# GNN and expert layers on one core: 70 instead of 77 edge groups in the dense part, a ring of 14 slots for the edge sums, three matrix scatter-adds per expert tile

## The chip, the cores and the metric

The kernel runs on one core of a Trainium2 chip. The metric is the device time of one execution in microseconds (us), and the median of several executions is compared. The program is written engine by engine: TensorE (PE) multiplies, VectorE (DVE) and ScalarE (ACT) work on rows, GpSimd (POOL) issues the indirect DMAs (gathers and scatter-adds), SyncE (SP) issues most of the plain DMAs.

## What is computed

```python
x (6250, 256); 100000 edges (src, dst, edge_weight), sorted by dst; dst is 6250*u*u, so low nodes have many edges
# layer 0, graph part: sum of weighted neighbours, two products with batch norm and relu, residual
agg = segment_sum(edge_vals[:, None] * x[edge_col], edge_row)
# layer 0, experts: router, top 2 of 8 experts, each LayerNorm -> 256x1024 -> gelu -> 1024x256, residual
# layer 1, graph part, twice (c1, c2), with the same edges:
h   = relu(x @ w1 + b1)
agg = segment_sum(ew[:, None] * h[src], dst)
h   = relu(batch_norm(agg @ w2 + b2))
# layer 1, experts: small shared MLP and top 2 of 4 small experts, residual
```

## The kernel before, in words

Edges are taken in NG = 196 groups of 512 (G = 4 tiles of 128). Nodes are held as rows in `X` (128 partitions x 50 tiles x 256), `A` is an area of the same size for work, and `T` holds columns. The stages run one after the other with a barrier between them, in the order of `build`.

`scattered_sum` (layer 0) makes the edge sums by scatter-adds: four per group on POOL (L582) into three copies of `node_sums`. Beside it, in the first 26 iterations of a loop over 6 groups, it also prepares "records": for each of the first groups a 128x128 matrix of edge weights between sources and destinations of each 128-edge piece, built on DVE (`side_prepare`, `side_picks`), mixed on PE and written to `rec_dram` by ACT. The records don't depend on node values. They serve both graph passes of layer 1.

The records are then added into `pair_dram` (a matrix source x destination, in two streams of columns, `STREAMS`) by POOL: four scatter-adds for each of the records `HALVES`, spread over six stages by the table `FEED` and issued by `add_pairs` (L177). In a stream an addition waits until the one before it has landed. `summed_product`, `norm_product`, `norm_to_rows`, `router`, `expert_ffn` and `combine_message` carry 2, 6, 6, 9, 49 and 6 records.

`expert_ffn` processes tiles of 256 tokens with a ring of SLOTS = 4: SP loads the weights of the tile's expert and, behind a wait for a free slot, a record; PE turns the tokens (L1230), multiplies (L2101, L2111); DVE scales; POOL's `tile` scatter-adds the result rows (L2030), gathers the tokens of four tiles later (L2026), and adds four matrices of one record between them:

```python
scatter(s, 0)
take(pool, in_ready[s])
gather(s, 0)
pairs(q, s, 0)
pool.wait_ge(y_out[s], q * 32 + 16)
scatter(s, 1)
pairs(q, s, 1)
gather(s, 1)
pairs(q, s, 2)
pool.wait_ge(y_out[s], q * 32 + 32)
pairs(q, s, 3)
```

`segment_sum` runs twice (layer 1). The first NA = 77 groups are replaced by the dense part: 50 `block_step`s on PE multiply node rows with the matrix rows of `pair_dram`. The other 119 groups go through a ring of RING = 7 slots: POOL gathers four tiles of `h_rows` (L1054), ACT scales them by the weights (L1070), PE multiplies with a 0/1 matrix (`products`, L1094) once for each node tile that the group touches, and DVE adds the result into `T` (L1147). ACT scales LEAD = 3 groups ahead of the refill of a slot. POOL fills a slot again when `idx_ready` says that DVE is done with it. Three block steps go with each round of seven groups (L1103 to L1105).

The `router` stage writes the token rows to `x_dram` (for the scatter-adds of `expert_ffn`) as the first thing on SP's queue behind its records, then the normalised rows `xn_rows` as they are made, then the gates. `combine_message` reads `x_dram` back into `X` and adds its share of the records.

## Time and profile before

| | before |
|---|---|
| median of 3 runs | 4832.23 us (4832.22 to 4843.71) |
| the profiled execution | 4828.0 us, of which the span is 4825.1 us |
| granted TensorE clock, mean | 0.896 of full speed |
| busy: PE, DVE, ACT, POOL | 3626.5, 2092.8, 1686.9, 2994.0 us |
| scatter-adds and gathers issued by POOL | 784 (layer 0), 312 (matrices), 952 (edge gathers), 208 (experts) |

The profile is one execution. "Busy" counts the time in which an engine executes. "Idle before, released by" says what ended an engine's wait; "issue" and an engine's own queue (POOLq L86) with 0.30 us stand for the queue's own work between two instructions.

### The profile page before, as it was taken

How to read it: one execution, taken by the hardware profiler on the slowest of the kernel's cores; microseconds unless marked ns; L12 is line 12 of the kernel's file. 1: busy time of each engine (PE TensorE's matmuls, PEld its weight loads, DVE VectorE, ACT ScalarE, POOL GpSimd, SP SyncE). 2: the span in 40 equal slices, each digit the busy share in tenths (PEclk: the TensorE clock that was granted, in tenths of full speed). 3: DMA queues.
4: the chain of work that ended last, by engine and by line, in shares of the span. 5: the costliest groups of instructions: out<-in, count | busy, mean ns of one | idle time of the engine just before them, and what ended most of it. 6: DMA issues, size and time to landing. Idle time of an engine off the chain costs nothing. (4 is left out here: it accounts for less than half of the span.)

```text
span 4825.1 us, 80886 instructions
## 1 busy us (share of the span) xinstructions
PE 3626.5 (75%) x18440; PEld 2929.7 (61%) x18447; DVE 2092.8 (43%) x5976; ACT 1686.9 (35%) x3989; POOL 2994.0 (62%) x2380
## 2 busy tenths in 40 slices
PE   3666666666676584699988858888886788885889
PEld 2555555555555462577777746677765667764667
DVE  6666666666665377211111113222334222235545
ACT  3333333333333254122222215333336333334543
POOL 4777777777778644566666656777741777770100
PEclk9788888888899797899999978999998899997999
DMA  8777777777776747677888845555533455540000
GB/s 267 130 130 135 129 127 134 129 129 130 128 101 88 141 131 150 164 193 191 200 201 196 219 121 154 163 162 162 162 88 106 148 164 160 162 135 18 14 18 23
DMA packets 504194, 664.11 MB, mean 138 GB/s; under 512 B 74076, under 2 KB 431648, under 8 KB 502025
## 3 DMA queue, kind: packets, MB, share of 16 engines
q0 software_dynamic: 225584, 284.52, 35.4%
q1 hardware_dynamic: 255913, 339.06, 22.4%
q10 hardware_dynamic: 22448, 38.04, 2.1%
q14 instruction: 195, 1.60, 0.1%
q8 instruction: 54, 0.88, 0.1%
HBM read 421.15 MB, written 240.25 MB: 137 GB/s over the span
## 5 line engine op out<-in xcount | busy, mean ns | idle before, releaser
L582 POOL DMA_INDIRECT node_sums<-T,scattered_sum_idx x760 | 1188.8, 1564 | 329.7 <-issue 193.3
L1054 POOL DMA_INDIRECT A<-h_rows,segment_sum_idx x952 | 935.3, 982 | 450.6 <-issue 251.3
L1094 PE MATMUL bank<-A 128*128 128x128 f32 x5120 | 670.1, 293 | 186.8 <-PEq L86 186.5
L1094 PEld LDWEIGHTS bank<-A 128*128 128x128 f32 x5120 | 651.3, 207 | 253.0 <-issue 252.3
L712 PE MATMUL bank<-X,T 128*128 x1952 | 606.9, 466 | 92.4 <-PEq L86 89.4
L706 PE MATMUL bank<-T 128*128 128x128 f32 x1952 | 339.5, 329 | 439.7 <-PEq L86 439.6
L1070 ACT ACTIVATE A<-A,segment_sum_edge 128x256 f32<-128x256 f32 x952 | 405.7, 496 | 718.9 <-DMA A<-h_rows,segment_sum_idx 718.9
L706 PEld LDWEIGHTS bank<-T 128*128 128x128 f32 x1952 | 301.1, 232 | 463.8 <-issue 459.3
L712 PEld LDWEIGHTS bank<-X,T 128*128 128x128 f32 x1952 | 443.7, 239 | 190.9 <-issue 119.7
L177 POOL DMA_INDIRECT pair_sums<-expert_ffn_record x196 | 305.0, 1556 | 222.6 <-POOLq L86 140.6
L1147 DVE TENSOR_TENSOR T<-T,bank 128x256 f32 x320 | 134.5, 420 | 638.8 <-DVEq L86 638.7
L2085 ACT ACTIVATE T<-bank,A 128x256 f32<-128x256 f32 x416 | 195.7, 474 | 513.7 <-ACTq L86 513.5
L609 ACT ACTIVATE T<-bank,rstd 128x512 f32<-128x512 f32 x244 | 167.6, 687 | 519.6 <-ACTq L86 519.6
L788 DVE SCALAR_TENSOR_TENSOR T<-T,edges,not_after 128x128 f32<-128x128 int16 x784 | 223.8, 348 | 183.5 <-DVEq L86 162.6
L1139 DVE TENSOR_TENSOR A<-iota,segment_sum_edge 128x512 f32<-128x512 f32 x238 | 165.3, 694 | 209.3 <-DVEq L86 204.9
L629 ACT ACTIVATE T<-bank 128x512 f32<-128x512 f32 x392 | 212.8, 595 | 105.9 <-ACTq L86 105.4
L798 DVE TENSOR_SCALAR T<-iota,edges 128x128 f32<-128x128 f32 x784 | 227.4, 370 | 23.0 <-issue 0.5
L2101 PE MATMUL bank<-A,T 128*128 128x256 f32 x832 | 196.6, 389 | 19.2 <-PEq L86 19.2
L1105 PE MATMUL bank<-A,segment_sum_step_h 128*128 128x512 f32 x400 | 205.7, 596 | 0.0
L2129 DVE SCALAR_TENSOR_TENSOR expert_ffn_gate<-T,rank 128x1 f32<-128x1 f32 x104 | 18.7, 221 | 429.0 <-DVEq L86 429.0
L2030 POOL DMA_INDIRECT x_rows<-A,expert_ffn_ring_out x104 | 160.8, 1546 | 69.7 <-DMA x_rows<-A,expert_ffn_ring_out 25.3
L1251 PE MATMUL bank<-T,w 128*128 (+1 forms) x800 | 189.4, 393 | 19.2 <-PEq L86 19.2
(377 smaller groups left out, 5763.4 us busy)
## 6 DMA issues: line engine op xcount, KB each, us to landing
T<-in_L_ffn_W SPq DMA_DIRECT2D x52, 1024.0 KB
A<-in_L_ffn_W SPq DMA_DIRECT2D x52, 1024.0 KB, 8.9
A<-pair_sums SPq DMA_DIRECT2D x100, 448.0 KB
T<-src_lanes SPq DMA_DIRECT2D x196, 128.0 KB, 3.4
pair_sums<-A SPq DMA_DIRECT2D x100, 224.0 KB
pair_records<-A ACTq DMA_DIRECT2D x78, 258.0 KB, 3.7
A<-node_sums SPq DMA_DIRECT2D x36, 512.0 KB, 7.2
A<-h_rows,segment_sum_idx POOLq DMA_INDIRECT x952
```

The source lines that it names most:

```text
L177: pool.indirect_dma_start(c.pair_dram[s], bass.IndirectOffsetOnAxis(ap=goal[:, j:j + 1], axis=0), f.slots[r][:, s, j * P:(j + 1) * P], Non ...
L582: pool.indirect_dma_start(c.sum_dram[at % COPIES], bass.IndirectOffsetOnAxis(ap=idx[:, h % LR, j:j + 1], axis=0), msg[:, h % LR * G + j, : ...
L629: ins = act.activation(msg[:, r * G + q * 2:r * G + q * 2 + 2, :].rearrange("p j d -> p (j d)"), out[s][q][:], ACT.Copy)
L706: mm = pe.matmul(mix[s][:, j * P:(j + 1) * P], picks[s][:, j, :], same[h % LR][:, j, :], start=True, stop=True)
L712: mm = pe.matmul(out[s][j // 2][:, j % 2 * D:(j % 2 + 1) * D], coef[p][:, j * P:(j + 1) * P], tile_at(c.X, b), start=(first and j % 2 == 0 ...
L788: ins = dve.scalar_tensor_tensor(same[r][:, j, :], lane[:, j * P:(j + 1) * P], c.edges[:, SRC, bass.ds(g * G + j, 1)], c.not_after[:], ALU ...
L798: ins = ts(picks[s][:, j, :], c.iota[:], key(j), c.edges[:, WEIGHT, bass.ds(g * G + j, 1)], ALU.is_equal, ALU.mult)
L1054: pool.indirect_dma_start(msg[:, h * G + j, :], None, c.h_dram, bass.IndirectOffsetOnAxis(ap=idx[:, h, j:j + 1], axis=0)).then_inc(landed[ ...
L1070: ins = act.activation(m, m, ACT.Identity, scale=edge[:, h, WEIGHT, j:j + 1])
L1094: mm = pe.matmul(acc[s][:, k * P:(k + 1) * P], msg[:, h * G + j, k * P:(k + 1) * P], hot[:, s, j, :], start=(j == 0), stop=(j == G - 1))
L1105: mm = pe.matmul(far[m][:, 0:WA[1] - 3 * P], h, rows[:, WA[0] + 3 * P:], start=first, stop=True, skip_group_check=True)
L2101: mm = pe.matmul(ph[k % 2][:, 0:TOK], w1[s][:, d, k * P:(k + 1) * P], xe[:, d, :], start=(d == 0), stop=(d == KD - 1))
```

## The change

1. `NQ` and `RING` go from 11 x 7 to 5 x 14: NA is 70 groups instead of 77, so each `segment_sum` gathers 126 groups instead of 119. `HALVES` goes from 78 to 70 records, the second stream is 6 column tiles wide instead of 7, and the records' side work in `scattered_sum` runs in 24 iterations instead of 26, with `side_picks` moved to the same step as `side_prepare`.
2. The ring of `segment_sum` has 14 slots: twelve lie in `X`, two in `A`. ACT scales six groups ahead. Six block steps go with each round of 14 groups.
3. Since the ring destroys `X`, the second `aggregate_product` reads the rows back from `x_dram` (`x_back`).
4. `FEED` is 5, 6, 6, 8, 37 and 8 records. `expert_ffn` has three additions per tile instead of four, in three record slots, and the last three records are loaded early into slots of their own.
5. In `router` the write of `x_dram` goes behind the writes of `xn_rows` and of the gates.

```diff
-RING = 7
-LEAD = 3
+RING = 14
+LEAD = 6
-NQ = 11
+NQ = 5
 NA = NQ * RING
-HALF = -(-NA // 2)
+HALF = NA // 2
-KG = 2 * HALF
+KG = -(-NA // SIDE) * SIDE
-STREAMS = ((0, 2), (1, 7))
+STREAMS = ((0, 2), (1, 6))
-FEED = {"summed_product": (0, 2), "norm_product": (2, 8), "norm_to_rows": (8, 14), "router": (14, 23),
-        "expert_ffn": (23, 72), "combine_message": (72, HALVES)}
+FEED = {"summed_product": (0, 5), "norm_product": (5, 11), "norm_to_rows": (11, 17), "router": (17, 25),
+        "expert_ffn": (25, 62), "combine_message": (62, HALVES)}
...
-            assert UN == 2 * SIDE and NJ <= KG // SIDE < LOOPS - 1
-            with eng.Fori(NJ, KG // SIDE + 1) as i:
-                for h in range(UN):
-                    ahead_of(i + (h + 1) // UN, (h + 1) % UN)
-                    now(i, h)
-                    side(i, h)
-            with eng.Fori(KG // SIDE + 1, LOOPS - 1) as i:
+            assert KG == SIDE * (NJ - 1) and UN == 2 * SIDE
+            with eng.Fori(NJ, LOOPS - 1) as i:
...
-        free = flat(c.A)
-        msg = carve(free, 0, (RING * G, D))
+        free, spare = flat(c.A), NB * D // (G * D)
+        msg = [carve(flat(c.X), h * G * D, (G, D)) if h < spare else carve(free, (h - spare) * G * D, (G, D)) for h in range(RING)]
...
-        SPREAD = ROUNDS - NQ - 2
-        LEFT = NB - DS * (SPREAD + 1)
+        PER = 6
+        SPREAD = (ROUNDS - NQ - 2) * PER // DS
+        EARLY = DS
+        LEFT = NB - EARLY - DS * SPREAD
...
+            if x_back:
+                for lo, hi in ((0, NB // 2), (NB // 2, NB)):
+                    sp.dma_start(flat(c.X)[:, lo * D:hi * D], token_rows(c)[:, lo * D:hi * D]).then_inc(x_in, 16)
+                sp.wait_ge(x_in, 32)
...
-            sp.dma_start(token_rows(c), flat(c.X)).then_inc(x_out, 16)
-            sp.dma_start(c.x_dram[0:SPARE, :], c.X[:, 0, :]).then_inc(x_out, 16)
...
             sp.dma_start(tokens[:, :, D:D + 2], c.pick[:]).then_inc(x_out, 16)
+            sp.dma_start(token_rows(c), flat(c.X)).then_inc(x_out, 16)
+            sp.dma_start(c.x_dram[0:SPARE, :], c.X[:, 0, :]).then_inc(x_out, 16)
...
-                pairs(q, s, 0)
+                pairs(q, 3 * s)
                 pool.wait_ge(y_out[s], q * 32 + 16)
                 pool.sem_inc(y_free[s], 1)
                 scatter(s, 1)
-                pairs(q, s, 1)
                 gather(s, 1)
-                pairs(q, s, 2)
+                pairs(q, 3 * s + 1)
                 pool.wait_ge(y_out[s], q * 32 + 32)
                 pool.sem_inc(y_free[s], 1)
-                pairs(q, s, 3)
+                pairs(q, 3 * s + 2)
...
             for s in range(SLOTS):
-                for k in range(4):
-                    add_pairs(pool, c, feed, 1 + FEED_STEPS * SLOTS + s, s, k, None)
+                for n in range(3 * s, 3 * s + 3):
+                    add_pairs(pool, c, feed, 1 + FEED_STEPS * RF + n // 4, RF + n // 4, n % 4, None)
```

## Rows read from the trace of the kernel before

**Rows 1.** Page, part 1: busy us, share of the span, instructions.
```profile
PE 3626.5 (75%) x18440; PEld 2929.7 (61%) x18447; DVE 2092.8 (43%) x5976; ACT 1686.9 (35%) x3989; POOL 2994.0 (62%) x2380
```
**Rows 2.** Edge gathers in each pass (ns min/median/max, first to last start); POOL's waits, pass one.
```profile
L1054 POOL DMA_INDIRECT A<-h_rows,segment_sum_idx x476: 942/946/1452, 2963.9 to 3573.3; - x159
...
L1054 POOL DMA_INDIRECT A<-h_rows,segment_sum_idx x476: 942/946/1463, 3718.9 to 4331.8; - x159
...
POOL A L1054 <- POOLq L86: 38.3, 72, 16.6
```
**Rows 3.** First `segment_sum`: busy us (instructions) of PE, PEld, DVE, ACT, POOL; clock; DMA; GB/s.
```profile
3060.00:3560.00 500.00, 430.93 (x2602) 356.68 (x2601) 145.37 (x265) 192.89 (x582) 381.72 (x389) 0.95 0.53 161
```
**Rows 4.** `expert_ffn`: PE turns the second, the sixth and the last tile (start, us).
```profile
1996.81 0.60 PE L1230 MATMUL bank<-ident,T 128*128 128x128 f32 x4
...
2056.57 0.60 PE L1230 MATMUL bank<-ident,T 128*128 128x128 f32 x4
...
2816.56 0.60 PE L1230 MATMUL bank<-ident,T 128*128 128x128 f32 x4
```
**Rows 5.** `expert_ffn`: POOL in one tile, in order of time [idle before, released by].
```profile
2200.35 1.54 POOL L2030 DMA_INDIRECT x_rows<-A,expert_ffn_ring_out  x1 [0.30 <-issue]
2202.20 1.02 POOL L2026 DMA_INDIRECT T<-xn_rows,expert_ffn_ring_in  x1 [0.30 <-issue]
...
2210.41 1.57 POOL L177 DMA_INDIRECT pair_sums<-expert_ffn_record  x1 [0.30 <-issue]
2215.51 1.54 POOL L177 DMA_INDIRECT pair_sums<-expert_ffn_record  x1 [3.54 <-DMA pair_sums<-expert_ffn_record]
2217.36 1.54 POOL L2030 DMA_INDIRECT x_rows<-A,expert_ffn_ring_out  x1 [0.30 <-DMA pair_sums<-expert_ffn_record]
```
**Rows 6.** End of `expert_ffn`: PE's last products; last scatter-adds of POOL's last two tiles.
```profile
2831.16 7.07 PE L2111 MATMUL bank<-A,T 128*128 128x256 f32 x32
...
2850.30 1.54 POOL L2030 DMA_INDIRECT x_rows<-A,expert_ffn_ring_out  x1 [2.97 <-DMA x_rows<-A,expert_ffn_ring_out]
...
2867.49 1.54 POOL L2030 DMA_INDIRECT x_rows<-A,expert_ffn_ring_out  x1 [3.04 <-DMA x_rows<-A,expert_ffn_ring_out]
```
**Rows 7.** `router`: eleventh and last (36th) addition on POOL; DVE's last work.
```profile
1915.76 1.81 POOL L177 DMA_INDIRECT pair_sums<-T  x1 [1.29 <-DMA pair_sums<-T]
...
1968.57 1.54 POOL L177 DMA_INDIRECT pair_sums<-router_record  x1 [0.74 <-DMA pair_sums<-router_record]
...
1950.73 0.54 DVE L1955 CAST in_idx<-router_over 128x112 int32<-128x112 f32 x1
```
**Rows 8.** `summed_product`: first and seventh addition, DVE's last work, one window (columns as in 3).
```profile
1673.53 1.88 POOL L177 DMA_INDIRECT pair_sums<-summed_product_record  x1 [16.20 <-POOLq L86]
...
1697.37 1.85 POOL L177 DMA_INDIRECT pair_sums<-summed_product_record  x1 [3.89 <-DMA pair_sums<-summed_product_record]
...
1735.42 0.16 DVE L1275 TENSOR_TENSOR affine<-pcol,affine 128x2 f32<-128x2 f32 x1
...
1705.00:1715.00 10.00, 10.00 (x57) 8.80 (x56) 9.00 (x20) 6.32 (x14) 0.00 (x0) 1.00 1.04 403
```
**Rows 9.** `combine_message`: its last addition, and SP's first DMA in `segment_sum`.
```profile
2945.69 1.54 POOL L177 DMA_INDIRECT pair_sums<-T  x1 [0.53 <-issue]
...
2961.88 0.35 SPq L1033 DMA_DIRECT2D segment_sum_step_h<-h_rows  x1
```
**Rows 10.** `scattered_sum`: POOL's scatter-adds (L582) with side work, and without it.
```profile
1100.00:1200.00 100.00, 75.48 (x50) 0.89 0.74 128
1450.00:1550.00 100.00, 83.22 (x55) 0.90 0.69 88
```
**Rows 11.** `scattered_sum`, 600 to 1000 us: instruction queue; DVE where its loop starts again.
```profile
q14 instruction: 41, 0.34, 0.3%
...
696.92 1.14 DVE L788 SCALAR_TENSOR_TENSOR T<-T,edges,not_after 128x128 f32<-128x128 int16 x4 [3.93 <-DVEq L86]
```
**Rows 12.** Second `aggregate_product`: all engines (columns as in 3).
```profile
4345.00:4395.00 50.00, 45.47 (x200) 37.81 (x200) 20.02 (x52) 20.97 (x50) 0.00 (x0) 0.94 0.00 0
```

More of the change, by code:

```diff
@@ L425, in run @@
         at = 2 * EPT
-        keys, local, weight, other_key = [af[:, at + i * KC:at + (i + 1) * KC] for i in range(4)]
-        absolute = sb("absolute", [P, KC])[:]
+        keys, local, weight, other_key, absolute = [af[:, at + i * KC:at + (i + 1) * KC] for i in range(5)]
         at = 6 * GE
@@ L468, in within, with in_order @@
             return nc.s_assert_within(b, 0, FULL, skip_runtime_bounds_check_because=CLAMPED)
-        def in_order(eng, ahead_of, now, after=lambda n: None, beside=lambda i, h: None, side=lambda i, h: None):
+        def in_order(eng, ahead_of, now, after=lambda n: None, beside=lambda i, h: None):
             ahead_of(0, 0)
@@ L551, in _ @@
             sp.wait_ge(record_out, 48)
-            sp.wait_ge(pairs_blanked, 16 * (2 + 5 * ZS))
+            sp.wait_ge(pairs_blanked, 16 * (2 + 4 * ZI))
         @block.gpsimd
@@ L694, in _ @@
                 act.sem_inc(record_out_of[r], 16)
-            in_order(act, ahead_of, now, lambda n: first_sum(3) if n == 1 else None, beside=beside, side=side_beside)
+            in_order(act, ahead_of, now, lambda n: first_sum(3) if n == 1 else None, beside=beside)
             act.wait_ge(x_read, 1)
@@ L775, in _ @@
             pe.wait_ge(centred, NB)
-            in_order(pe, ahead_of, now, beside=beside, side=lambda i, h: side_beside(h))
+            in_order(pe, ahead_of, now, beside=beside)
         @block.vector
@@ L886, in beside @@
                         side_prepare(i, h // 2)
-                    else:
-                        side_picks(i, h // 2)
                 elif h == 1:
@@ L935, in _ @@
             statistics()
-            in_order(dve, ahead_of, now, beside=beside, side=beside)
+            in_order(dve, ahead_of, now, beside=beside)
     stage(nc, run, "scattered_sum")
@@ L1008, in run @@
         WA = [w * P for t0, w in STREAMS]
-        step_h = sb("step_h", [P, DS, D])
-        step_rows = [free[:, RING * G * D + 3 * GE + d * sum(WA):][:, 0:sum(WA)] for d in range(DS)]
+        step_h = carve(free, at + 3 * GE, (DS, D))
+        step_rows = [free[:, at + 3 * GE + DS * D + d * sum(WA):][:, 0:sum(WA)] for d in range(DS)]
         near, far = c.ps[3:5], c.ps[5:7]
@@ L1037, in step @@
                     at += WA[s]
-            for d in range(DS):
-                step(d, d)
+            for t in range(EARLY):
+                step(t, t % DS)
             load_w(sp, c, next_slot, next_w)
-            with sp.Fori(1, SPREAD + 1) as q:
+            with sp.Fori(0, SPREAD) as q:
                 for d in range(DS):
-                    step(q * DS + d, d)
-            for d in range(LEFT):
-                step(DS * (SPREAD + 1) + d, d)
+                    step(q * DS + (EARLY + d), (EARLY + d) % DS)
+            for t in range(NB - LEFT, NB):
+                step(t, t % DS)
         @block.gpsimd
@@ L1114, in group @@
                         products(h, 2)
-            assert STREAMS == ((0, 2), (1, 7)) and 1 <= LEFT <= DS
-            for d in range(DS):
-                block_step(d, first=(d == 0))
+            assert STREAMS == ((0, 2), (1, 6)) and 1 <= LEFT <= RING and PER % DS == 0
+            for t in range(EARLY):
+                block_step(t % DS, first=(t == 0))
             with pe.Fori(first_round(pe), NQ + 1) as q:
@@ L1129, in _ @@
                 if h < LEFT:
-                    block_step(h, after=block_summed if h == LEFT - 1 else None)
+                    block_step((NB - LEFT + h) % DS, after=block_summed if h == LEFT - 1 else None)
         @block.vector
@@ L1987, in run @@
         first_record, last_record = FEED["expert_ffn"]
-        feed = Feed(sem, [sb(f"record{r}", [P, 2, REC])[:] for r in range(SLOTS)])
-        assert last_record - first_record == 1 + (FEED_STEPS + 1) * SLOTS and FEED_STEPS < STEPS_MIN - 1
+        RF = FEED_SLOTS
+        feed = Feed(sem, [sb(f"record{r}", [P, 2, REC])[:] for r in range(2 * RF)])
+        assert last_record - first_record == 1 + (FEED_STEPS + 1) * RF and FEED_STEPS < STEPS_MIN - 1 and 3 * SLOTS == 4 * RF
         @block.sync
@@ L2018, in _ @@
                     load(q * SLOTS + s, s)
-            for s in range(SLOTS):
-                take(sp, feed.rec_free[s])
-                load_record(sp, c, feed, first_record + 1 + FEED_STEPS * SLOTS + s, s)
         @block.gpsimd
@@ L2200, in _ @@
                 if n >= 2:
-                    for r in range((n - 2) * 2, (n - 1) * 2):
+                    for r in range((n - 2) * 3, min((n - 1) * 3, last_record - first_record)):
                         load_record(sp, c, feed, first_record + r, r)
```

93 lines of the change are left out of this document (51 added, 42 removed).

## Prediction, made before the changed kernel was run

> **What bounds the kernel now.** The page comes first: PE is busy for 75% of the span, POOL for 62%, and neither says much, since the stages have different limits [rows 1]. So I read the gathers and POOL's waits, then windows by stage, then single tiles in order of time.
>
> In `segment_sum` POOL sets the pace. The 476 gathers of the first pass start between 2963.9 and 3573.3 us: 609.4 us over 475 steps, 1.283 us each; the second pass gives 612.9 / 475 = 1.290 us [rows 2]. The reader is to see that POOL never waits for a slot: of its 38.3 us of queue waits 16.6 are the wait before the stage, and the other 71 last 0.3 us, which is issue. A gather takes 0.95 us, some 1.45, and 0.30 us lies between two. PE is busy for 431 of 500 us [rows 3], near the limit but behind the gathers.
>
> In `expert_ffn` the bound changes. The first tiles run at PE's pace: four take from 1996.81 to 2056.57 us, 14.94 us each. All 50 steps from the second tile to the last take 819.75 us, 16.40 each [rows 4]. The tile of rows 5 shows why: from one first scatter-add to the next are 17.01 us in which POOL has eight DMAs, none waiting for PE's `y_done`; before the fourth matrix addition POOL waits 3.54 us for a landing [rows 5]. POOL is behind by the ring's four tiles, and PE waits for gathers. At the end POOL goes on for some 34 us after PE, at 17.19 us per tile [rows 6].
>
> In `router` POOL ends last too: DVE is done at 1951.3 us, POOL's last addition starts at 1968.57 [rows 7]. In `scattered_sum` it is POOL again (50 scatter-adds in 100 us with side work, 55 without [rows 10]); in `summed_product` DVE and PE end last, since POOL's few additions are over early [rows 8].
>
> **The change, part by part.**
>
> *Edge gathers.* 9 rounds x 14 slots x 4 = 504 per pass instead of 476, so 28 more in each. 28 x 1.283 + 28 x 1.290 = **+72 us**. What could pay for them inside the stage is a wait of POOL, and there is none [rows 2]: a ring twice as long and scaling six ahead buy nothing where POOL is never kept waiting for a slot. ACT has 14 fetches ahead instead of 7, behind a first gather that POOL issues after the first fetch, so nothing. PE gets 7 more groups but a block step loses a column tile; PE is hidden behind POOL as before. The last round has five block steps in its first five groups; nine groups follow in which PE catches up, where it had five before. Bounds: all hidden, 0; at 0.95 + 0.45 + 0.30 each, +95. Taken: +72, the row's own pace.
>
> *Expert tiles.* Three additions instead of four: 1.54 + 0.30 = 1.85 us less of POOL's work. 17.01 - 1.85 = 15.2 if the landing wait stays; the wait is for additions of a stream, and with one addition fewer they stand further apart, so it should shrink, and then PE's 14.94 is the floor. A scatter-add is now followed by a gather and one addition before it is awaited, 5.0 us instead of 6.9, so a new wait of up to 2 us for `y_out` takes part of that place. I take 15.1: 50 x (16.40 - 15.1) = **-65 us**. Bounds: 14.94 gives -73; no change of pace gives 0. On SP's queue the record's load now stands behind only three of four weight loads, and its wait for a record slot holds back the next weights by some tenths of a tile; they are loaded four tiles ahead, so PE doesn't see it.
>
> *Expert tail.* Each of the last four tiles has three additions instead of four: 4 x 1.85 = 7 us less. POOL also enters the tail on time instead of with what is left of its lag, and no record has to be loaded then. The last tile's own work (two scatter-adds one after the other, 2867.49 less 2850.30 without four additions, about 9.3 us) and some 4 us of landing and lag then remain behind PE's end of 2838.2, instead of 34: **-18 us** (bounds -7 and -24).
>
> *Router.* Four additions fewer: the last 25 steps take 52.8 us, 2.11 each [rows 7], so -8. And `x_dram`'s 6.4 MB no longer run beside the first additions (ten steps up to 1915.76, of which the DMA writes make most wait); the write moves behind the gates, still well before DVE's end. It costs the additions as much there, but the first 13 us are free for them: -6. DVE's end at 1951.3 is the floor, 17 us below POOL's. **-14 us** (bounds -8 and -17).
>
> *Other records.* `summed_product` has 20 additions instead of 8. While the reads saturate the DMA engines (403 GB/s), six steps take 23.8 us [rows 8]; by 1715 twelve are done, eight more at 2.11 us end at 1732, landed at 1737, against DVE's 1735.6; three more record loads push the third part of the sums back by 2 us. **+3** (0 to +8). `combine_message` has 32 instead of 24: eight more at 2.11 us from 2945.69 on end at 2962.6, landed at some 2967, where SP now begins the next stage at 2961.88 [rows 9]: **+5** (+3 to +8).
>
> *`scattered_sum`.* Two iterations (48 scatter-adds) lose their side work: at 2.00 against 1.82 us each [rows 10] **-9 us**. Against it, DVE does `side_prepare` and `side_picks` in one go; POOL is three groups of rows behind and covers some microseconds. Bounds -15 and +20 (the burst costs 1 us in every group).
>
> *Reading `X` back.* 6.4 MB at 403 GB/s [rows 8] are 16 us, in a stage in which PE is busy for 45 of 50 us and the DMA engines and POOL do nothing [rows 12]: 0. Uncovered it would be +16.
>
> *Sum.* 72 - 65 - 18 - 14 + 3 + 5 - 9 = **-26 us** against the profiled execution's own 4828.0: 4802. The median of the runs is 4.2 us above that execution, so 4806 as a median.
>
> **A rule that speaks against the doubled ring.** In `scattered_sum` the instruction queue moves 41 packets in 400 us, about five per iteration, and where the loop starts again DVE stands 3.93 us [rows 11]: that body doesn't stay loaded. In `segment_sum` the body of seven groups shows no such stops, and fourteen groups have twice the code. The Trainium skill (Runtime: NRT & Kernel Launch, section Instruction fetch mechanics) says that a taken branch to a target outside the pages held forces a fetch before execution goes on, and rows 11 agree. What it would do here is a rival below, priced from the row alone.
>
> **The rivals.**
>
> 1. *The experts' landings set the pace, not the number of additions* (slower). POOL's wait before the last addition of a tile grows by what the addition saved, because scatter-adds, matrices and 2 MB of weights share the DMA engines. Then the tile stays at 16.4, the tail saves 7: 72 + 0 - 7 - 14 + 3 + 5 - 9 = +50, 4882. The point from which it decides: a tile above 15.7 us makes the kernel slower than before. For it: the 3.54 us wait is a landing. Against: the early tiles ran at 14.94 with POOL still adding four matrices per tile at its own pace. Chance 0.10.
> 2. *The extra gathers cost nothing* because something else than POOL's issue paces them (PE at 431 of 500 us): -98, 4734. Against: no wait on POOL. Chance 0.05.
> 3. *The doubled loops are loaded again in every round.* 8 returns x 2 passes x 3.9 us = 63 us if POOL or PE stands and nothing covers it: +37, 4869. On DVE, busy for 145 of 500 us, or with 14 slots ahead, it is covered. Chance 0.07.
> 4. *The single burst of side work holds up the scatter-adds:* 144 groups x 0.2 us or more; with the upper bound of +20 in place of -9 the sum is +3, no change: 4835. Chance 0.10.
>
> **How the numbers follow.** My forecast has 0.68. Its own range, with the pace of a tile between 14.94 and 15.5 and the small terms at either end, is 4785 to 4825. For 8 in 10 the range must reach to rival 4 and to half-kept expert savings: 4775 to 4842. This measurement tells 0.3% (14.5 us) from no change: below 4817.7 is faster. Of my forecast's 0.68, 0.57 lies there, 0.10 in between and 0.01 above; rival 2 adds 0.05 to faster; rivals 1 and 3 add 0.17 to slower; rival 4 gives 0.07 to the same and 0.03 to slower. Faster 0.62, same 0.17, slower 0.21.
>
> **What would show it.** 504 gathers per pass at 1.28 to 1.29 us, 645 to 650 us from first to last, with POOL's waits again only 0.3 us; expert tiles 15.0 to 15.3 us apart and no longer a wait of PE for gathered rows; POOL's last scatter-add of the stage within 12 us of PE's end; the router's last addition near 1954 on this kernel's clock; reads into `X` landed before PE's products of the second `aggregate_product` end. The prediction is wrong if tiles stay above 15.7 us, if gathers start faster than every 1.25 us, or if PE or DVE stand 4 us at each return of the gather loop and POOL waits for a slot there.

## The result, and the profile after

The changed kernel takes 4801.12 us as the median of 5 runs (4797.0 to 4816.57), the kernel before 4832.23 us (4829.95 to 4843.71): ratio 0.9939, 95% interval 0.9926 to 0.9951. That is 0.6% faster. The forecast was 4806 us with "faster" as the likeliest case. The profiled execution of the changed kernel took 4809.04 us (span 4807.0), 8 us above its median; of before 4828.0 (span 4825.1). So the trace has 18.1 us to explain, not the 31 between the medians, against -26 in the forecast.

Page of the changed kernel, part 1 (as [rows 1]):

```profile
PE 3606.4 (75%) x18654; PEld 2972.0 (62%) x18655; DVE 2087.6 (43%) x5941; ACT 1713.0 (36%) x4061; POOL 3000.4 (62%) x2404
```

The shares hardly move. The edge gathers by line, in pass one (first two lines) and two (last two), and POOL's waits in pass one (as [rows 2]):

```profile
L1051 POOL DMA_INDIRECT X<-h_rows,segment_sum_idx x432: 942/946/1469, 2872.5 to 3512.4; - x144
L1051 POOL DMA_INDIRECT A<-h_rows,segment_sum_idx x72: 942/946/1434, 2933.7 to 3523.1; - x72
...
L1051 POOL DMA_INDIRECT X<-h_rows,segment_sum_idx x432: 942/946/1454, 3667.5 to 4305.4; - x144
L1051 POOL DMA_INDIRECT A<-h_rows,segment_sum_idx x72: 942/946/1428, 3729.0 to 4315.7; - x72
...
POOL X L1051 <- issue: 101.4, 333, 0.3
POOL X L1051 <- POOLq L87: 34.9, 99, 5.0
```

504 gathers per pass: 650.6 us over 503 steps is 1.293 us each, 648.2 in pass two 1.289. POOL waits 0.3 us at a time, as before: the longer ring removed no wait, there was none. In `expert_ffn`, PE's turns of the second and last tile, and POOL around one tile (as [rows 4, 5]):

```profile
1982.71 0.60 PE L1227 MATMUL bank<-ident,T 128*128 128x128 f32 x4
...
2729.06 0.60 PE L1227 MATMUL bank<-ident,T 128*128 128x128 f32 x4
...
2205.66 1.54 POOL L2036 DMA_INDIRECT x_rows<-A,expert_ffn_ring_out  x1 [4.99 <-DMA x_rows<-A,expert_ffn_ring_out]
2207.51 1.02 POOL L2032 DMA_INDIRECT T<-xn_rows,expert_ffn_ring_in  x1 [0.30 <-issue]
2208.83 1.57 POOL L178 DMA_INDIRECT pair_sums<-expert_ffn_record  x1 [0.30 <-issue]
2210.70 1.55 POOL L178 DMA_INDIRECT pair_sums<-expert_ffn_record  x1 [0.30 <-issue]
```

50 steps take 746.35 us, 14.93 each; of four tiles three take 14.60 us and one, where the loops start again, 15.95. No turn after the first waits for gathered rows. POOL's long wait now stands before the second scatter-add of a tile, for the landing of the first. The means over tiles 9 to 41 say what POOL's tile is made of: before, 16.75 us from first scatter-add to first scatter-add, 13.75 of them eight DMAs with 0.30 us of issue each and 3.0 a landing wait before the fourth addition; now 15.08 us, 11.9 for seven DMAs and 3.1 for landing waits (2.3 before the second scatter-add, 0.6 before the third addition, 0.2 before the first). At the stage's end (as [rows 6]; the two last scatter-adds of the last two tiles and the additions between) and in `router` (its last addition, as [rows 7]):

```profile
2755.92 1.55 POOL L2036 DMA_INDIRECT x_rows<-A,expert_ffn_ring_out  x1 [3.08 <-DMA x_rows<-A,expert_ffn_ring_out]
2760.59 1.54 POOL L178 DMA_INDIRECT pair_sums<-expert_ffn_record  x1 [3.12 <-DMA x_rows<-A,expert_ffn_ring_out]
2762.43 1.54 POOL L178 DMA_INDIRECT pair_sums<-expert_ffn_record  x1 [0.30 <-issue]
2764.59 1.54 POOL L178 DMA_INDIRECT pair_sums<-expert_ffn_record  x1 [0.62 <-POOLq L87]
2766.44 1.54 POOL L2036 DMA_INDIRECT x_rows<-A,expert_ffn_ring_out  x1 [0.30 <-issue]
2770.97 1.54 POOL L2036 DMA_INDIRECT x_rows<-A,expert_ffn_ring_out  x1 [2.99 <-DMA x_rows<-A,expert_ffn_ring_out]
...
1955.00 1.54 POOL L178 DMA_INDIRECT pair_sums<-router_record  x1 [0.65 <-issue]
```

The reads of `X` are issued at 4328.68 us and land within 17.2 us, under PE's products, which go on to 4374: they cost nothing. The span cut at the same events in both traces (the forecast for both passes of `segment_sum` is +72 us, put half and half):

| stretch | before, us | after, us | difference | forecast |
|---|---|---|---|---|
| up to `scattered_sum`'s last scatter-add | 1655.8 | 1645.0 | -10.8 | -9 |
| to the first addition of `norm_product` | 84.5 | 89.1 | +4.6 | +3 |
| to the last addition of `norm_to_rows` | 106.7 | 111.1 | +4.4 | 0 |
| to POOL's first gather of `expert_ffn` (`router`) | 127.2 | 115.3 | -11.9 | -14 |
| to PE's turn of the second tile | 22.6 | 22.2 | -0.4 | 0 |
| 50 expert tiles | 819.75 | 746.35 | -73.4 | -65 |
| PE's last turn to POOL's last scatter-add | 50.9 | 41.9 | -9.0 | -18 |
| to the first edge gather (`combine_message`) | 96.4 | 101.5 | +5.1 | +5 |
| to the first gather of pass two | 755.0 | 795.0 | +40.0 | +36 |
| to the end | 1106.2 | 1139.5 | +33.3 | +36 |
| sum | | | -18.1 | -26 |

The +4.4 of the third row belongs to no part of the change: in the traces of the twelve experiments, whose additions there are the same, the stretch takes 106.0 to 107.5 us in seven and 108.4 to 111.0 in five.

### The profile page after: what moved, and what is told of

It is laid out like the page before. It is cut to its first block and busy times, and to the rows that moved or that the text cites. A ratio compares the mean times of both kernels' runs of the same rounds, so it can differ in the third digit from the quotient of the medians.

```text
span 4807.0 us, 80989 instructions
## 1 busy us (share of the span) xinstructions
PE 3606.4 (75%) x18654; PEld 2972.0 (62%) x18655; DVE 2087.6 (43%) x5941; ACT 1713.0 (36%) x4061; POOL 3000.4 (62%) x2404
## 5 line engine op out<-in xcount | busy, mean ns | idle before, releaser
L582 POOL DMA_INDIRECT node_sums<-T,scattered_sum_idx x760 | 1185.8, 1560 | 324.7 <-issue 196.0
L1051 POOL DMA_INDIRECT X<-h_rows,segment_sum_idx x864 | 852.7, 987 | 411.1 <-POOLq L87 208.5
L1091 PE MATMUL bank<-A,X 128*128 128x128 f32 x4640 | 622.3, 297 | 202.6 <-PEq L87 202.4
L1091 PEld LDWEIGHTS bank<-A,X 128*128 128x128 f32 x4640 | 601.2, 211 | 246.1 <-issue 228.2
L1067 ACT ACTIVATE X<-X,segment_sum_edge 128x256 f32<-128x256 f32 x864 | 368.2, 496 | 656.0 <-DMA X<-h_rows,segment_sum_idx 656.0
L1144 DVE TENSOR_TENSOR T<-T,bank 128x256 f32 x336 | 141.2, 420 | 670.0 <-DVEq L87 669.8
L178 POOL DMA_INDIRECT pair_sums<-expert_ffn_record x148 | 230.7, 1559 | 119.0 <-POOLq L87 54.9
L2105 PE MATMUL bank<-A 128*128 128x256 f32 x832 | 193.0, 386 | 0.0
L2430 POOL TENSOR_SCALAR A<-X,rstd,shift 128x256 f32<-128x256 f32 x50 | 32.8, 667 | 251.4 <-POOLq L87 232.1
```

Source lines behind the costliest of these rows:

```text
L178: pool.indirect_dma_start(c.pair_dram[s], bass.IndirectOffsetOnAxis(ap=goal[:, j:j + 1], axis=0), f.slots[r][:, s, j * P:(j + 1) * P], Non ...
L582: pool.indirect_dma_start(c.sum_dram[at % COPIES], bass.IndirectOffsetOnAxis(ap=idx[:, h % LR, j:j + 1], axis=0), msg[:, h % LR * G + j, : ...
L1051: pool.indirect_dma_start(msg[h][:, j, :], None, c.h_dram, bass.IndirectOffsetOnAxis(ap=idx[:, h, j:j + 1], axis=0)).then_inc(landed[h], 16)
L1067: ins = act.activation(m, m, ACT.Identity, scale=edge[:, h, WEIGHT, j:j + 1])
L1091: mm = pe.matmul(acc[s][:, k * P:(k + 1) * P], msg[h][:, j, k * P:(k + 1) * P], hot[:, s, j, :], start=(j == 0), stop=(j == G - 1))
L2105: mm = pe.matmul(ph[k % 2][:, 0:TOK], w1[s][:, d, k * P:(k + 1) * P], xe[:, d, :], start=(d == 0), stop=(d == KD - 1))
```

## The experiments

Twelve kernels ran. In the diffs, `...` stands for lines left out. Each ratio is to the kernel before on the same chip; the changed kernel's own is 0.9939.

**The old ring with 70 groups.** The segment stage as in the kernel before, dense part and records as in the changed one:

```diff
-RING = 14
-LEAD = 6
+RING = 7
+LEAD = 3
...
-NQ = 5
+NQ = 10
...
-        msg = [carve(flat(c.X), h * G * D, (G, D)) if h < spare else carve(free, (h - spare) * G * D, (G, D)) for h in range(RING)]
+        msg = [carve(free, h * G * D, (G, D)) for h in range(RING)]
...
-        aggregate_product(nc, c, c.w[1], (c.w_in[1], 48), col("L1_gnn_c2_b2"), col("L1_gnn_c2_g"), col("L1_gnn_c2_b"), x_back=True)
+        aggregate_product(nc, c, c.w[1], (c.w_in[1], 48), col("L1_gnn_c2_b2"), col("L1_gnn_c2_g"), col("L1_gnn_c2_b"))
...
```

> The changed kernel with the old ring: 70 groups in the dense part as there, but 7 slots in A, three groups scaled ahead, X not used and not read back. My theory: POOL's issue sets the pace of the edge sums and never waits for a slot, so the ring of 14 bought nothing: both passes keep 504 gathers, the time is that of the changed kernel within 5 us (ratio to the kernel before 0.993 to 0.995). Rival a, the longer ring helps: then POOL waits for slots here and the gathers slow from 1.29 to 1.31 us or more, +20 us or more against the changed kernel. Rival b, the doubled loop costs something: then the gathers return from 1.293 us to the 1.283 of the kernel before, -10 us over both passes against the changed kernel, ratio 0.991 to 0.992.

Measured: 4802.39 us, ratio 0.9953 (0.9939 to 0.9966). Its gathers in both passes:

```profile
L1051 POOL DMA_INDIRECT A<-h_rows,segment_sum_idx x504: 942/946/1467, 2861.2 to 3510.4; - x168
...
L1051 POOL DMA_INDIRECT A<-h_rows,segment_sum_idx x504: 942/946/1472, 3654.3 to 4303.3; - x168
```

649.2 and 649.0 us from first to last, against 650.6 and 648.2 with 14 slots. One pair of traces could hide the 10 us of rival b, but pass one takes 644.2 to 651.6 us in the ten traces with 14 slots, and seven slots lie in the middle of that. Ring, area and reading back together change nothing that can be measured; rivals a and b both fall.

**77 groups with three additions per tile.** The kernel before with the changed kernel's `expert_ffn` and `router`, and the records placed so:

```diff
-FEED = {"summed_product": (0, 2), "norm_product": (2, 8), "norm_to_rows": (8, 14), "router": (14, 23),
-        "expert_ffn": (23, 72), "combine_message": (72, HALVES)}
+FEED = {"summed_product": (0, 5), "norm_product": (5, 11), "norm_to_rows": (11, 17), "router": (17, 25),
+        "expert_ffn": (25, 62), "combine_message": (62, HALVES)}
```

> The kernel before, its 77 groups in the dense part and its ring of 7 kept, with the changed kernel's expert stage (three additions per tile), router and summed_product records; the eight records that then lack a place go to combine_message, 16 there instead of 8. It parts the exchange from the ring. My theory: a group costs either 8 gathers of 1.28 us in the edge sums or four matrix additions of 2.1 us where POOL ends a stage last, nearly the same: -72 us of gathers against the changed kernel, +67 us in combine_message (32 additions x 2.11), +11 in scattered_sum and its side work, together +6, 0 to +15 us against the changed kernel, still 12 to 25 us faster than the kernel before. Rival: the additions in combine_message overlap work that bounds it today; then it costs under +40 and this version beats both by 20 us or more.

Measured: 4816.76 us, ratio 0.9974 (0.9965 to 0.9983); span 4813.6 against 4796.4 with 70 groups and the same ring. The 17.2 us by the same events: gathers -36.7 and -36.2, `combine_message` +72.1 for 32 additions (2.25 us each), `scattered_sum` +10.2, `expert_ffn` +7.4, the rest +0.4. The exchange is nearly even, as the theory had it: 72.9 us of gathers against 72.1 of additions and some 10 of side work. The difference is 17 us in these traces (10 by the two ratios), above the 6 expected and the bound of 15; of the 11 us more, 7.4 stand in `expert_ffn`, whose code is that of the changed kernel: three late turns of PE (17.55, 17.12 and 16.36 us after the one before). They come when POOL is some 46 us behind PE; the later experiments look for what puts it there.

**One addition in four left out.** The kernel before; each record's fourth addition in `expert_ffn` isn't made (49 in all, so part of the sum is missing):

```diff
-                add_pairs(pool, c, feed, q * SLOTS + (1 + s), s, k, (s - 1) % SLOTS)
+                if k < 3:
+                    add_pairs(pool, c, feed, q * SLOTS + (1 + s), s, k, (s - 1) % SLOTS)
```

> The kernel before with the fourth matrix addition of each record left out in the expert stage (49 additions left out in all, so part of the sum is missing); nothing else changed. My theory: POOL's count of DMAs alone set the tile: 50 tiles at 14.9 to 15.1 us instead of 16.4, -65 to -75 us there, and a further -7 to -10 in the last four tiles: 4743 to 4756 us for the profiled execution. Rival, the order within the tile did it (the changed kernel gathers before its second addition, this one after it): then the tiles stay above 15.4 here. Rival, landings pace the tile: they stay at 16.2 or more.

Measured: 4741.36 us, just under the 4743 to 4756 expected. PE's turns of the second and the last tile, and the two scatter-adds of one tile on POOL:

```profile
1991.75 0.60 PE L1231 MATMUL bank<-ident,T 128*128 128x128 f32 x4
...
2738.04 0.60 PE L1231 MATMUL bank<-ident,T 128*128 128x128 f32 x4
...
2196.35 1.54 POOL L2032 DMA_INDIRECT x_rows<-A,expert_ffn_ring_out  x1 [2.92 <-POOLq L86]
...
2201.40 1.55 POOL L2032 DMA_INDIRECT x_rows<-A,expert_ffn_ring_out  x1 [0.30 <-issue]
```

746.29 us for 50 steps, 14.93 each: one addition fewer is enough for the 73 us, whatever the order, and both rivals fall. It is not the count of DMAs alone, though. Issue alone takes 13.75 us for eight, less than PE's tile; what held PE up was that with the 3.0 us landing wait before the fourth addition, and that wait goes when the addition goes. POOL now waits 2.8 us per tile in the mean before the first scatter-add, for PE's tile, and hardly for landings. The tail takes 36.6 us instead of 50.9.

**No additions in `expert_ffn`.** The changed kernel; the 148 additions of the stage aren't made, so that part of the sum is missing. In the loops:

```diff
-                    tile(q, s, pairs)
+                    tile(q, s, skip)
...
```

> The changed kernel with all 148 matrix additions of the expert stage left out (that part of the sum is missing). My theory: at three additions per tile PE is already the bound, so the 50 steps stay at 14.9 us each (746 us); only the tail gets shorter: POOL's last scatter-add about 36 us after PE's last turn instead of 42, since the landing waits stay, -6 to -14 us in all. Rival: POOL still sets part of the pace through the DMA engines that both use; then the steps fall below 14.8 us and the time by another 10 us or more.

Measured: 4791.03 us, 50 steps in 746.36 us as expected, a tail of 29.2 us instead of 41.9, where 36 was expected. PE is the floor at 14.93 us per tile. The additions cost the tail 12.7 us, by their own time and by POOL's coming late: at the last tile before the tail it is 25.4 us behind PE here and 36.0 in the changed kernel. The whole execution is 18 us shorter than that of the changed kernel, 12.4 of it in `expert_ffn`.

**The tail.** Twelve additions behind the scatter-adds, in front of the wait for landing:

```diff
...
             for s in range(SLOTS):
-                for n in range(3 * s, 3 * s + 3):
-                    add_pairs(pool, c, feed, 1 + FEED_STEPS * RF + n // 4, RF + n // 4, n % 4, None)
                 take(pool, y_done[s])
                 for t in range(2):
                     scatter(s, t)
+                    if s < SLOTS - 1:
+                        late(4 * s + 2 * t, 4 * s + 2 * t + 2)
                     pool.wait_ge(y_out[s], last * 32 + 16 * (t + 1))
```

> The changed kernel with the twelve matrix additions of the last four expert tiles put behind a tile's scatter-adds, in front of the wait for their landing, four with each of the first three tiles and none with the last; in the changed kernel three stand ahead of each tile's first scatter-add and both landings are waited for bare. My theory: POOL's tail tiles of 15.2 us hold two bare landing waits of some 2 to 3 us each, which the additions can fill: POOL ends 8 to 12 us earlier behind PE's last product (11 us behind it, not 20), ratio 0.992 to 0.993 against the kernel before. Rival: the additions' own landings under the DMA load pace the tail, then it stays within 2 us of the changed kernel.

Measured: 4789.01 us, ratio 0.9926 (0.9913 to 0.994). The third tile's additions and the last tile's scatter-adds:

```profile
2740.23 1.54 POOL L178 DMA_INDIRECT pair_sums<-expert_ffn_record  x1 [0.74 <-DMA pair_sums<-expert_ffn_record]
2742.08 1.54 POOL L178 DMA_INDIRECT pair_sums<-expert_ffn_record  x1 [0.30 <-issue]
2746.58 1.54 POOL L2036 DMA_INDIRECT x_rows<-A,expert_ffn_ring_out  x1 [2.96 <-POOLq L87]
2751.14 1.54 POOL L2036 DMA_INDIRECT x_rows<-A,expert_ffn_ring_out  x1 [3.02 <-DMA x_rows<-A,expert_ffn_ring_out]
...
2645.82 0.66 PE L1227 MATMUL bank<-ident,T 128*128 128x128 f32 x4 [2.36 <-DMA T<-xn_rows,expert_ffn_ring_in]
```

PE's last turn is at 2721.93 us, so the tail takes 29.2 us, as if it had no additions: POOL now waits for PE's last tile, and both landings are hidden but those of that tile. The theory holds (-12.7 us, a little more than the 8 to 12 expected). The last line is another matter: PE waits for gathered rows (2.8 us in two places), and the 50 steps take 752.9 us.

**Eight additions between the loops.** The version above, one record fewer in `router` and in `combine_message`:

```diff
...
+            late(0, 4 * GAP)
             with pool.Fori(FEED_STEPS, last) as q:
...
```

> The version with the additions behind the tail's scatter-adds, and two records (eight matrix additions) moved out of the ends of two stages: one from router (7 records, 28 additions), one from combine_message (7 records), both into the expert stage between its two loops, where a round of four tiles follows that has no additions. My theory: POOL ends router 8 us behind VectorE and ends combine_message too, so four additions fewer in each give back 6 to 8 us and some 5 us; the eight additions in the expert stage cost POOL 15 to 17 us ahead of a round in which it has about 5 us to spare per tile, with gathered rows four tiles ahead, so PE does not wait: -11 to -15 us against the version without it, ratio 0.989 to 0.991 against the kernel before. Rival: POOL is already level with PE in the last rounds, the burst makes PE wait for gathered rows and the tail ends later by as much as the eight additions: then no gain or a loss of up to 5 us.

Measured: 4797.27 us, ratio 0.9938 (0.9921 to 0.9955). `router` gives 6.5 us (107.1 against 113.6, to the first gather) and `combine_message` 5.8 (95.7 against 101.5), as expected, and `expert_ffn` takes 15.3 more. The rival holds, and the loss is larger than it said; PE's wait:

```profile
PE bank L1228 <- DMA T<-xn_rows,expert_ffn_ring_in: 17.9, 2, 15.7
```

So POOL has no time in hand there. I took POOL's lag (its first scatter-add of a tile less PE's turn of the same tile) from the traces at each third tile. In the changed kernel it goes from 34.5 us at the first tile to 42.6 at the 43rd; in the tail version to 46.8 at the 40th, and the first late turn of PE follows there. Where one addition in four is left out it falls to 25 to 27 us, and without additions it is 25 to 27 all along.

**The wait behind the third addition.** The tail version with this loop:

```diff
                 scatter(s, 1)
-                gather(s, 1)
                 pairs(q, 3 * s + 1)
+                gather(s, 1)
+                pairs(q, 3 * s + 2)
                 pool.wait_ge(y_out[s], q * 32 + 32)
                 pool.sem_inc(y_free[s], 1)
-                pairs(q, 3 * s + 2)
```

> The version with the additions behind the tail's scatter-adds, and the order of a tile in the expert loops changed: after the second scatter-add stand addition, gather, addition and then the wait for its landing; there the wait stands before the third addition. What it is to tell: in the kernel before with one addition left out, where all additions of a tile stand ahead of its waits, POOL's first scatter-add of a tile stood 25 to 27 us behind PE's turn of the same tile; in the changed kernel 34 us at first and 40 to 46 near the end, and from about 46 PE waits for gathered rows. My theory: that is the third addition behind the wait; with the new order the lag falls to 25 to 28 us, no PE turn is later than 16 us after the one before, and the runs that stood there gain up to 7 us: 0 to -7 us against the version without it, ratio 0.991 to 0.993. Rival: the lag comes of the DMA engines' load or of the record's stream order; then it still grows beyond 35 us.

Measured: 4793.52 us, ratio 0.9923 (0.991 to 0.9936); the lag still grows, to 42.5 us at the 43rd tile, and one turn is 17.13 us after the one before. The ratio lies where I put it, but my theory falls: the place of the wait is not it. With eight additions between the loops:

> The last one, and again eight additions moved from router and combine_message into the expert stage between its two loops, which cost 15 us of PE's standing when POOL came there 45 us behind. My theory: POOL now comes there with 20 us of room, the eight additions take up to 26, and PE stands 0 to 5 us instead of 20; router gives 7 us, combine_message 6: -8 to -13 us against the last one, ratio 0.988 to 0.991 against the kernel before. Rival: the room is not there (the lag stays above 35 us), and PE stands 10 us or more again: no gain.

Measured: 4797.89 us, ratio 0.9927 (0.9914 to 0.994), PE's wait for gathered rows 8.6 us. The expert stage (first gather to last scatter-add) takes 810.6 us, 9.9 more than without them. That is no gain, as the rival said; PE's late turns cost 11.4 us, and the lag before them was 32 to 37 us. And with twelve:

> The same with twelve additions between the loops, the third record taken from summed_product (4 records, 16 additions). My theory: the twelve take 30 to 36 us, 10 to 15 more than the room, so PE stands 5 to 15 us more than with eight, and summed_product gives back 3 to 5: 0 to +10 us against the version with eight. Rival: POOL catches up in the round without additions and PE's slots of gathered rows cover it all: then -3 to -5 us.

Measured: 4796.7 us, ratio 0.9931 (0.9918 to 0.9944); the expert stage takes 818.8 us, 8.2 more than with eight, and the stretch up to the first addition of `norm_product` 85.5 us, 3.8 less: +4.4 from the stages, within the theory's 0 to +10. The medians (-1.2 us) can't tell this.

What differed between the kernel with a lag of 25 us and these was on SP's queue. SP's weight loads (1 MB each; the two weights of a tile) and record loads in the changed kernel:

```profile
2188.43 0.39 SPq L164 DMA_DIRECT2D expert_ffn_record<-pair_records  x1
2190.19 0.41 SPq L2002 DMA_DIRECT2D T<-in_L_ffn_W  x1
2190.70 0.44 SPq L2003 DMA_DIRECT2D T<-in_L_ffn_W  x1
2193.91 0.39 SPq L2002 DMA_DIRECT2D T<-in_L_ffn_W  x1
2194.40 0.42 SPq L2003 DMA_DIRECT2D T<-in_L_ffn_W  x1
2209.91 0.39 SPq L164 DMA_DIRECT2D expert_ffn_record<-pair_records  x1
2211.22 0.40 SPq L2002 DMA_DIRECT2D A<-in_L_ffn_W  x1
...
2230.05 0.40 SPq L2002 DMA_DIRECT2D A<-in_L_ffn_W  x1
```

and in the kernel before with one addition in four left out:

```profile
2186.61 0.39 SPq L164 DMA_DIRECT2D expert_ffn_record<-pair_records  x1
2188.26 0.40 SPq L1998 DMA_DIRECT2D T<-in_L_ffn_W  x1
...
2202.44 0.39 SPq L1998 DMA_DIRECT2D T<-in_L_ffn_W  x1
...
2217.09 0.40 SPq L1998 DMA_DIRECT2D A<-in_L_ffn_W  x1
...
2232.38 0.40 SPq L1998 DMA_DIRECT2D A<-in_L_ffn_W  x1
```

SP stands before each record load until POOL has emptied a slot, with the next weights queued behind it. With four records per four tiles this happens once per tile and the weights leave every 14.2 to 15.3 us. With three, one tile has no record: two tiles' weights leave 3.7 us apart, the others after 17, 19 and, for the next tile without one, 20 us. Bunching by itself does no harm: without any additions the loads leave after 6.8, 14.6, 17.4 and 21.0 us, and the lag stays at 25 to 27.

**Records two tiles later on SP's queue.** The version with eight additions between the loops, and:

```diff
...
-                    if s >= 1:
-                        take(sp, feed.rec_free[s - 1])
-                        load_record(sp, c, feed, q * RF + (first_record + s), s - 1)
+                    if s in records:
+                        r = (s + 1) % SLOTS
+                        take(sp, feed.rec_free[r])
+                        load_record(sp, c, feed, (q - (r > 0)) * RF + (first_record + 1 + r), r)
...
```

> The version with eight additions between the loops and the wait behind the third addition, and on SP's queue of the expert stage each record's load two tiles later (behind the weights of the fourth, first and second tile of a round, not of the second, third and fourth). What stands behind it: in the changed kernel SP waits for a free record slot in front of the next weights, and of four weight loads two are issued 3.7 us apart (2190.19 and 2193.91 us) and the others 17 and 19 us later, while with one load per record and tile (the kernel before less one addition) they stand 12.7 to 14.6 us apart; POOL's lag behind PE was 25 us there and 34 to 46 here. My theory: the two bunched loads of 2 MB each lengthen the landings that POOL waits for; with the later records the weights are evenly spread, the lag before the last rounds falls to 25 to 30 us, the eight additions between the loops then cost PE 0 to 3 us instead of 13, and the version is 8 to 13 us faster than that without this change: ratio 0.989 to 0.991 against the kernel before. Rival: the bunching has no part in POOL's lag (it stays above 34 us by the tenth round), the stand of PE stays above 10 us, ratio 0.992 to 0.993.

Measured: 4788.52 us, ratio 0.9897 (0.988 to 0.9915), the lowest ratio of all. In the loop `records` is (0, 1, 3). Weights in its trace, and PE's wait:

```profile
2181.24 0.39 SPq L2003 DMA_DIRECT2D T<-in_L_ffn_W  x1
...
2195.83 0.40 SPq L2003 DMA_DIRECT2D A<-in_L_ffn_W  x1
...
2210.43 0.40 SPq L2003 DMA_DIRECT2D A<-in_L_ffn_W  x1
...
2226.51 0.40 SPq L2003 DMA_DIRECT2D T<-in_L_ffn_W  x1
...
PE bank L1228 <- DMA T<-xn_rows,expert_ffn_ring_in: 4.4, 1, 4.4
```

The weights leave every 14.6 to 16.1 us, at PE's pace, and the lag falls to 29 to 32 us in the middle and 26.7 at the 43rd tile, where it was 36.3 without this edit. So it is shown that the order on SP's queue makes a good part of the lag. How it does so is not: I had put it to longer landings behind two bunched loads, but POOL's mean idle time before the second scatter-add of a tile (tiles 9 to 40) is 2.98 us with this edit and 3.27 without, against 0.36 in the kernel before less one addition, and the median from issue to landing of these scatter-adds (2150 to 2600 us) is 7.0 us with it and 6.2 without. The waits only spread more evenly over the four tiles of a round: 3.9, 3.0, 1.9 and 3.1 us instead of 0.3, 5.2, 3.1 and 4.4. The gain in the stage is smaller than I said: 805.8 us against 810.6, -4.8; PE's two late turns still cost 6.9 us (11.4 before), not 0 to 3. The ratio fell by 0.3% (14 us, above the 8 to 13 expected; the medians differ by 9.4), but the two were run apart, each beside its own runs of the kernel before, and the intervals touch; the expert stage's traces carry 4.8 us of it.

**Side work in two goes** (`scattered_sum`). The changed kernel with:

```diff
                     if h % 2 == 0:
                         side_prepare(i, h // 2)
+                    else:
+                        side_picks(i, h // 2)
```

> The changed kernel with VectorE's side work of a group in two goes again: side_prepare beside the even group, side_picks beside the odd one, as in the kernel before; ScalarE's and TensorE's part stays where the change put it. My theory: the single burst costs POOL nothing, since the scatter-adds are three groups of rows behind it: last scatter-add within 4 us of the three runs of this code so far (1636 to 1645 us on the profile's clock, 1500 to 1509 us after the first), total within 5 us of the changed kernel. Rival: the burst costs up to 1 us in every group of three, and the split gives back 5 to 15 us of scattered_sum: first to last scatter-add under 1497 us.

Measured: 4800.95 us, ratio 0.9951 (0.9937 to 0.9965). Its scatter-adds, and the changed kernel's:

```profile
L582 POOL DMA_INDIRECT node_sums<-T,scattered_sum_idx x760: 1538/1541/2587, 136.7 to 1638.5; - x190
```

```profile
L582 POOL DMA_INDIRECT node_sums<-T,scattered_sum_idx x760: 1538/1540/2480, 136.3 to 1645.0; - x190
```

1501.8 us against 1508.7, and 1498.2 to 1512.1 in the other traces with the single burst. The burst costs nothing that shows. In the three traces with 77 groups of side work the stretch is 1512.8 to 1516.6, in the mean 9.6 us longer than in the eleven with 70.

**The write of `X` first in `router`.** The changed kernel with the two writes in front again:

```diff
+            sp.dma_start(token_rows(c), flat(c.X)).then_inc(x_out, 16)
+            sp.dma_start(c.x_dram[0:SPARE, :], c.X[:, 0, :]).then_inc(x_out, 16)
             tokens = c.xn_dram.rearrange("(p t) d -> p t d", t=NB)
...
-            sp.dma_start(token_rows(c), flat(c.X)).then_inc(x_out, 16)
-            sp.dma_start(c.x_dram[0:SPARE, :], c.X[:, 0, :]).then_inc(x_out, 16)
```

> The changed kernel with the write of X to x_dram first on the router's queue again; its 32 matrix additions stay. My theory, from the terms of the prediction: the four additions fewer gave 8 us of the router's 11.8, the moved write the other 3 to 6: POOL's last addition of the stage 3 to 6 us later against the stage's start, +3 to +6 us in all. Rival: the write costs the additions the same wherever it stands (13.7 us of landing wait behind the moved one): then the last addition stays within 2 us, and the additions' count made the whole gain.

Measured: 4799.37 us, ratio 0.9944 (0.9928 to 0.9961). From the last addition of `norm_to_rows` to the last of `router`: 112.0 us here, 109.8 in the changed kernel and 107.9 to 110.8 in six others with its order and 32 additions; 121.6 in the kernel before with 36; 101.0 to 102.7 in four with 28. The order is worth 1 to 4 us, at the theory's lower end or below. Four additions are worth 7 to 8 between 32 and 28, and 9.6 between 36 and 32 with the write first in both. The total can't tell this.

## Why the prediction was right, step by step

**Edge gathers: right.** +73.3 us for +72. A gather's pace is POOL's own (1.281 to 1.295 us in all fourteen traces), so 28 more cost 28 times that, and neither seven slots more nor scaling six ahead can return any of it. The old ring with 70 groups shows it.

**Expert tiles: POOL's pace right, the term 8 us too small.** I took 15.1 us per tile. That is POOL's own pace: 15.08 us in the mean from the 9th to the 41st tile, with landing waits as long as before (3.1 us per tile) where I had expected them to shrink. The step that was wrong is that PE would feel it. PE's tile is 14.93 us and gathered rows lie four tiles ahead, so POOL's lag grows by 0.14 us per tile (36.5 to 41.0 us over these 32 tiles), and PE first stands when it reaches some 44 to 46. The changed kernel ended its additions just short of that.

The wait of up to 2 us that I added, for the second scatter-add's landing before the third addition, is 0.6 us in the mean; the 4.99 us in the tile shown is for the first scatter-add's landing, a wait that the code had before and that cost nothing there.

On SP's queue I wrote that waiting for a record slot holds back the next weights by some tenths of a tile. It holds them back by half a tile to one and a half: in the tiles from the 9th to the 40th they leave 32 to 47 us after PE's turn of the tile whose slot they refill, and 24.4 to 26.1 us after it with the records two tiles later. With eight additions between the loops in both, that edit takes the lag at the 43rd tile from 36.3 to 26.7 us. In the trace of the changed kernel itself the lag was free up to the tail; in three of the five other traces with these loops and additions the 50 steps take 6.5 to 8.7 us more.

**Expert tail: mis-sized, -9.0 instead of -18.** The step said that POOL enters the tail on time and ends within 12 us of PE. It ends 20 us behind PE's last products. POOL was 36.0 us behind PE at the last tile before the tail instead of some 25, and the three additions still stand ahead of the scatter-adds while two landings are waited for bare, so that a tail tile takes POOL 15.2 us where PE needs 14.60 and nothing is made up. The kernel before less one addition has a tail of 36.6 us with three additions per tile, and POOL is 25.3 us behind PE ahead of it: by that, some 5 us of the miss are the late entry and 4 the tail's own work. (The last tile's own work is 9.8 us by the prediction's rows, 17.19 less 4 x 1.85, not 9.3.) Without additions the tail is 29.2 us, and with all twelve in the landing waits it is 29.2 us too.

**Router: right in sum, split otherwise.** -11.9 for -14: some 8 to 10 from four additions, for which I had 8, and 1 to 4, not 6, from the moved write.

**Small terms: right.** `summed_product` +4.6 for +3, `combine_message` +5.1 for +5, `scattered_sum` -10.8 for -9 (-9.6 in the mean of all traces), `X` read back 0.

**The rivals.** Landings that hold the expert tile at 16.4 us whatever the number of additions are out by the kernel with one addition in four left out, free gathers by the old ring with 70 groups, the burst of side work by its splitting. The doubled loops: over the same 600 us of pass one the two instruction queues move these packets with 14 and with 7 slots (the changed kernel first):

```profile
q8 instruction: 10, 0.16, 0.1%
q14 instruction: 4, 0.03, 0.0%
```

```profile
q8 instruction: 3, 0.05, 0.0%
q14 instruction: 1, 0.01, 0.0%
```

Some more code is fetched, but POOL's pace does not change (650.6 and 649.2 us). The rule of the Trainium skill (Runtime: NRT & Kernel Launch, section Instruction fetch mechanics) weighed ahead of the result had nothing to charge for on the engine that sets this stage's end. Nor do the engines behind it stand longer: between 2960 and 3500 us DVE's waits for its queue before L1144 come to 279.9 us with 14 slots and 282.3 with seven (longest 7.2 and 5.8), PE's before L1091 to 89.8 and 97.4 (longest 4.3 and 3.4), and none of POOL's is over 0.3.

The sum was 8 us off in the profile: the tiles 8 too small and the tail 9 too large, the router 2, and 4.4 us of `norm_to_rows` that move from trace to trace. That tiles and tail cancel (-82.4 for -83) is in part one cause, since lateness that PE doesn't feel in the tiles is paid in the tail, and in part luck: the lag stopped just short of where PE stands. That the median fits so closely (4801 for 4806) is luck too, since the profiled executions give -18 us and the medians -31.

## What to carry to other kernels

When work is moved between two stages in which the same engine ends last, price it on both sides first: seven groups are 56 gathers of 1.28 to 1.29 us or, here, 32 additions of 2.1 to 2.25 us and their side work, so the exchange is nearly even wherever POOL is the bound, and pays only where the engine drops below another's pace (16.40 to 14.93 us per tile). A longer ring is worth nothing if the producer never waits for a slot; look for that wait before paying with memory. Look also at what is queued behind a wait for a free slot on a DMA queue, and put small work between a scatter and the wait for its landing rather than ahead of the scatter: that was worth 12.7 us in the tail, where POOL ends the stage, and in the loops, where PE does, it did not take the lag away. An engine slightly slower than the one it feeds costs nothing until its lead is used up, so read its own pace and its lag, not only the other engine's waits.

## What the runs showed of the hardware that I had not expected

PE's tile of 14.60 us repeats within 0.01 us for hundreds of microseconds once nothing else is in its way, and the tile in which the loops start again takes 1.35 us more (15.95 us), 16 us over twelve rounds. In that tile PE waits 1.22 us for its queue between its first eight products and the next 24; which engine's loop it waits for was not told apart, and no experiment here tried to remove it. Identical stages differ between traces by more than the medians' intervals: the stretch in front of `scattered_sum`'s last scatter-add ends between 1634 and 1648 us with the same code, so differences under 5 us were read within a stage, never from the total.
